# Token routing of a two-part mixture of experts in groups of 512 tokens, the second time inside the attention's last steps

## The reference

```
x = x + 0.5 * ffn(layernorm(x))
x = x + attention(layernorm(x))
x = x + 0.5 * ffn(layernorm(x))        # the same weights as the first

ffn(x):   logits = x @ gate_w                       # 256 x 8 experts
          probs = softmax(logits); take the best 2 of 8, weights made to sum to 1
          for each token and chosen expert e:  silu(x @ w1[e]) * (x @ w3[e]) @ w2[e]
attention(x): a gated delta rule with 16 key heads and 32 value heads of 128, a causal
          convolution of 4 taps ahead of it, a gated norm behind it, and a projection W_out
```

## Time and profile before

| | |
|---|---|
| median of 3 runs | 2922.49 us (2917.46 to 2924.52) |
| profiled execution | 2920.82 us, its span 2919.1 us |
| mean granted TensorE clock | 0.962 of full speed |
| TensorE matmul busy | 2688.0 us, 92% of the span |
| VectorE busy | 1930.2 us, 66% |
| ScalarE busy | 1394.6 us, 48% |
| GpSimd busy | 679.9 us, 23% |

### The profile page before, as it was taken

How to read it: one execution, slowest core, us unless ns; L and a number is a source line. 1 busy time by engine, 2 the same in 40 slices (tenths; PEclk the granted TensorE clock), 3 DMA queues, 4 the chain that set the end, 5 groups by cost and what they waited for, 6 DMA issues and landing times. The chain is left out here.

```text
span 2919.1 us, 58298 instructions
## 1 busy us (share of the span) xinstructions
PE 2688.0 (92%) x19346; PEld 1992.1 (68%) x19347; DVE 1930.2 (66%) x3648; ACT 1394.6 (48%) x4441; POOL 679.9 (23%) x937
## 2 busy tenths in 40 slices
PE   4899997558999999999999999999999995899997
PEld 4566665335777777777777777777777774566665
DVE  5122222799999999999999999999977544322221
ACT  0111111435766667666666676676765551111111
POOL 0222221331232231321322322222221101122221
PEclk7999998889999999999999999999999996799999
DMA  4133322355645555555554554554653313132322
GB/s 164 46 81 101 78 52 56 117 172 181 194 146 165 178 159 168 164 164 165 161 178 149 172 165 158 179 163 153 185 142 94 101 55 126 28 91 72 102 65 47
DMA packets 378409, 374.79 MB, mean 128 GB/s; under 512 B 213360, under 2 KB 293744, under 8 KB 378160
## 3 DMA queue, kind: packets, MB, share of 16 engines
q1 hardware_dynamic: 363184, 351.08, 38.6%
q0 software_dynamic: 14976, 20.46, 4.3%
HBM read 234.87 MB, written 138.67 MB: 128 GB/s over the span
## 5 line engine op out<-in xcount | busy, mean ns | idle before, releaser
L548 PE MATMUL f_ps_up<-f_wbuf,f_xgT 128*128 x1248 | 499.8, 544 | 5.2 <-issue 3.2
L643 DVE TENSOR_TENSOR f_h<-f_h,f_ps_up 128x448 f32<-128x448 f32 x156 | 96.9, 621 | 471.6 <-ACT f_h L617 471.6
L617 ACT ACTIVATE f_h<-f_ps_up 128x448 f32<-128x448 f32 x156 | 84.8, 543 | 635.6 <-PE f_ps_up L548 635.6
L548 PEld LDWEIGHTS f_ps_up<-f_wbuf,f_xgT 128*128 128x128 f32 x1248 | 231.4, 192 | 189.5 <-issue 185.0
L1641 DVE SCALAR_TENSOR_TENSOR at_qk<-at_bank,at_taps_qk,at_qk 128x510 f32<-128x510 f32 (+2 forms) x384 | 281.9, 744 | 36.0 <-ACT at_qk L1512 26.9
L1641 DVE SCALAR_TENSOR_TENSOR at_vT<-at_bank,at_taps_v,at_vT 128x510 f32<-128x510 f32 (+2 forms) x384 | 280.4, 744 | 36.3 <-ACT at_vT L1519 27.3
L1314 PE MATMUL at_bank<-xnT,at_w_qk 128*128 128x512 f32 x512 | 254.6, 621 | 25.1 <-DVE at_qk L1641 21.5
L1890 POOL TENSOR_SCALAR at_small<-at_small 128x4 f32<-128x4 f32 x64 | 15.8, 247 | 1119.3 <-ACT at_squares L1546 1119.3
L515 POOL DMA_INDIRECT sums<-f_y,f_row_of x78 | 123.7, 1586 | 584.1 <-DVE f_y L654 579.4
L570 PE MATMUL f_ps_y<-f_wbuf,f_hT 128*128 x1092 | 248.8, 379 | 1.6 <-DVE f_hT L647 1.6
L1339 PE MATMUL at_bank<-at_w_vz,xnT 128*128 128x256 f32 x1024 | 243.5, 381 | 7.3 <-DVE at_vT L1641 7.2
(11 more groups left out here) (231 smaller groups left out, 5626.6 us busy)
## 6 DMA issues: line engine op xcount, KB each, us to landing
f_wbuf<-in_L_ffn_w_dram SPq DMA_DIRECT2D x48, 896.0 KB, 6.9
at_steps_e<-steps_kept SPq DMA_DIRECT2D x64, 512.0 KB, 6.7
mt_kept<-at_mt_made SPq DMA_DIRECT2D x64, 512.0 KB, 4.1
pt_kept<-at_pt_made SPq DMA_DIRECT2D x64, 512.0 KB, 3.1
at_mt<-mt_kept SPq DMA_DIRECT2D x64, 512.0 KB, 4.0
at_pt<-pt_kept SPq DMA_DIRECT2D x64, 512.0 KB, 4.6
ks_kept<-at_ks_made SPq DMA_DIRECT2D x64, 256.0 KB, 2.7
qk_kept<-at_qk SPq DMA_DIRECT2D x64, 256.0 KB, 2.7
```

The costliest lines, as they stand in the source:

```text
L548: last = te.matmul(ps_up[hf][w][:, 0:MH], xgT[b][:, k, :], wbuf[:, bass.ds(off + (w * WSIZE + k * M + hf * MH), MH)], start=(k == 0), stop ...
L643: v.tensor_tensor(part, part, ps_up[hf][1][:, 0:MH], ALU.mult).then_inc(h_ready, 1)
```

## The change

**Routing in groups.** `build_norm` and its block go. A class `Router` holds the pieces of norm, gate and choice for a group g of 512 tokens (four tiles): `stats` and `shift` on VectorE, `root` on GpSimd, `turn` and `logits` on TensorE, `copy` (both halves of `xnT`) and `exp` on ScalarE, `top` and `pick` on VectorE. Their small buffers now belong to the program. x is loaded in four DMAs, each with its own semaphore, the gate right after them, and the block of constants no longer waits for x.

**First part** (`routed` is False): the pieces run inside the routing block, as a pipeline of four groups. SP stores rows and x by group, and loads expert 1's weights after them.

**Second part** (`routed` is True): the pieces are steps of the walk, for the last key head's four units only; `AFTER` grows from 3 to 5 with the new entries of `STAGE`, so two steps are added at the end. The normalized rows stand in `mt_made` and `pt_made`, whose last use is over; transposes go to `inv_bank`, logits to `gen[0]` and `gen[2]`. SP stores rows and x by unit in the walk and waits for them at its end. The routing block of the second part then begins with the weights of experts 0 and 1 and the cast of `best_f`.

**Turned lists**: the list product loads `in_tile` (78 columns) and streams `at_place` (128), so the result has 78 rows and 128 columns. ScalarE copies it to SBUF (`listed`), and TensorE transposes it back.

**Orders**: all five tables of the drain are new. The front's tables stand twice in the file, with the same content. `tab["b"]` shares memory with `tab["g"]`.

```
-            sp.dma_start(x[:], x_dram.rearrange("b (c p) d -> p (b c) d", p=P)).then_inc(c["x_loaded"], 16)
+            for g in range(4):
+                sp.dma_start(x[:, 4 * g:4 * g + 4, :], x_dram[2 * g:2 * g + 2].rearrange("b (c p) d -> p (b c) d", p=P)).then_inc(c["x_loaded"][g], 16)
+            sp.dma_start(c["gate"][:], gate_w.rearrange("(k p) e -> p k e", p=P)).then_inc(c["gate_loaded"], 16)
...
-            pool.wait_ge(c["x_loaded"], 16)
...
+class Router:
...
+    def shift(self, dve, g):
+        v, c = self.nc.vector, self.c
+        dve.wait_ge(self.moments_done, 4 * g + 4)
+        dve.wait_ge(self.rstd_done, 2 * g + 2)
+        for t in self.tiles(g):
+            v.tensor_scalar(self.xn(g)[:, t - 4 * g, :], self.x[:, t, :], c["mv"][:, t, 0:1], c["rstd"][:, t:t + 1],
+                            ALU.subtract, ALU.mult).then_inc(self.xn_ready, 1)
...
+    def turn(self, pe, g):
+        pe.wait_ge(self.xn_ready, 4 * g + 4)
+        at_least(pe, self.xnT_ready, 2 * (g - self.pairs + 1))
+        for k in range(KD):
+            for t in range(4):
+                last = self.nc.tensor.transpose(self.turned[g % self.pairs][k][:, P * t:P * t + P],
+                                                self.xn(g)[:, t, P * k:P * k + P], self.c["ident"][:])
+            last.then_inc(self.turned_ready, 1)
...
+    def logits(self, pe, g):
+        pe.wait_ge(self.c["gate_loaded"], 16)
+        pe.wait_ge(self.xnT_ready, 2 * g + 2)
+        at_least(pe, self.shifted, g - 1)
...
+    def exp(self, act, g):
+        part = self.c["probs"][:, 4 * g:4 * g + 4, :]
+        act.wait_ge(self.shifted, g + 1)
+        self.nc.scalar.activation(part, part, ACT.Exp).then_inc(self.exp_done, 1)
...
@@ routing block, SP @@
+                    if routed:
+                        weight_loads(sp, 1, w1, w2, w3, wbuf, loaded)
+                        return
+                    for g in range(4):
+                        part = slice(512 * g, 512 * g + 512)
+                        sp.wait_ge(router.xn_ready, 4 * g + 4)
+                        sp.dma_start(rows_in[part, :].rearrange("(t p) d -> p t d", p=P), router.xn(g)).then_inc(rows_stored, 16)
+                        sp.wait_ge(c["x_loaded"][g], 16)
+                        sp.dma_start(sums[part, :].rearrange("(t p) d -> p t d", p=P), x[:, 4 * g:4 * g + 4, :]).then_inc(sums_begun, 16)
+                    weight_loads(sp, 1, w1, w2, w3, wbuf, loaded)
@@ routing block, TensorE @@
+                    if not routed:
+                        router.turn(pe, 0)
+                        for g in range(1, 4):
+                            router.turn(pe, g)
+                            router.logits(pe, g - 1)
+                        router.logits(pe, 3)
...
-                            last = nc.tensor.matmul(ps_token[:], at_place[:, i, :], in_tile[:, i],
+                            last = nc.tensor.matmul(ps_listed, in_tile[:, i].rearrange("p k t -> p (k t)"), at_place[:, i, :],
                                                     start=(i == 0), stop=(i == 2 * NT - 1))
-                    last.then_inc(tokens_summed, 1)
+                    last.then_inc(lists_summed, 1)
+                    pe.wait_ge(lists_copied, 1)
+                    nc.tensor.transpose(spare[0][:, 0:2 * TILES], listed[:],
+                                        c["ident"][0:2 * TILES, 0:2 * TILES]).then_inc(tokens_summed, 1)
@@ routing block, ScalarE @@
+                    act.wait_ge(lists_summed, 1)
+                    nc.scalar.copy(listed[:], ps_listed).then_inc(lists_copied, 1)
@@ routing block, VectorE @@
+                        for g in range(4):
+                            dve.wait_ge(c["x_loaded"][g], 16)
+                            router.stats(dve, g)
+                            if g:
+                                router.shift(dve, g - 1)
+                        router.shift(dve, 3)
+                        for g in range(4):
+                            router.top(dve, g)
+                            router.pick(dve, g)
@@ attention @@
+    "sums_out": -3, "ln_stats": -3, "ln_root": -3,
+    "ln_shift": -4, "rows_out": -4, "ln_turn": -4, "ln_copy": -4,
+    "logits": -5, "gate_exp": -5, "pick": -5,
...
+DRAIN_ACT_ORDER = (("weigh", 0), ("gate_qk", 0), ("copy_state",), ("norm",), ("from_state",), ("y_copy", 0),
...
+DRAIN_DVE_ORDER = (("from_state",), ("inv_x", 32), ("conv_qk", 0), ("ln_shift",), ("conv_qk", 1), ("blocks", 0),
+                   ("add", 0), ("shape",), ("add", 1), ("conv_v", 2), ("conv_v", 3), ("scan",), ("inv_x", 64),
...
+                def rows_out(u):
+                    if u[0] != NK - 1:
+                        return
+                    sp.wait_ge(router.xn_ready, 4 * u[1] + 4)
+                    sp.dma_start(rows_in[UT * u[1]:UT * u[1] + UT, :].rearrange("(t p) d -> p t d", p=P), router.xn(u[1])).then_inc(rows_kept[u[1] % 2], 16)
...
+                def ln_shift(u):
+                    if u[0] != NK - 1:
+                        return
+                    if u[1] < 2:
+                        for k in range(2):
+                            dve.wait_ge(s["pt_spilled" if u[1] else "mt_spilled"][k], 16 * (UNITS // 2))
+                    else:
+                        dve.wait_ge(router.turned_ready, 2 * (u[1] - 1))
+                        dve.wait_ge(rows_kept[u[1] % 2], 16)
+                    router.shift(dve, u[1])
```

More of the change, by code:

```diff
@@ L222, in weight_loads, with build_ffn @@
         eng.dma_start(dst.rearrange("p (k m) -> p k m", k=src.shape[1]), src).then_inc(loaded[e % 2], 16)
-def build_ffn(nc, c, x, xnT, gate_w, w1, w2, w3, rows_in, sums, prefix, finish):
+def build_ffn(nc, c, x, xnT, routed, w1, w2, w3, rows_in, sums, prefix, finish):
     ctx = ExitStack()
@@ L441, in _ @@
                 def _(pool):
+                    if not routed:
+                        for g in range(4):
+                            router.root(pool, g)
                     nc.gpsimd.iota(columns_i[:], [[1, P]], base=0, channel_multiplier=0).then_inc(numbers_made, 1)
@@ L683, in build @@
             ("zeros", [P, D], F32), ("iota_i", [P, TILES + 1], I32), ("iota", [P, TILES + 1], F32))}
-        for name in ("x_loaded", "constants_made", "out_stored"):
+        c.update({name: r.sb("rt_" + name, shape, dtype) for name, shape, dtype in (
+            ("stats", [P, NT, 6], F32), ("mv", [P, NT, 2], F32), ("rstd", [P, NT], F32), ("gate", [P, KD, E], F32),
+            ("row", [P, NT], F32), ("probs", [P, NT, E], F32), ("best", [P, NT, 8], F32), ("best_at", [P, NT, 8], U32))})
+        for name in ("gate_loaded", "constants_made", "out_stored"):
             c[name] = r.dma_sem(name)
+        c["x_loaded"] = [r.dma_sem(f"x_loaded{k}") for k in range(4)]
         c["x_back"] = [r.dma_sem(f"x_back{k}") for k in range(4)]
@@ L976 @@
-DRAIN_ACT_ORDER = (("weigh", 0), ("copy_state",), ("from_state",), ("y_copy", 0), ("y_copy", 1), ("norm",),
-                   ("turn", 1), ("turn", 0), ("conv_v", 2), ("conv_v", 3), ("conv_qk", 0), ("gate_v", 2), ("inv_n",),
-                   ("weigh", 1), ("ks",), ("gate_v", 3), ("conv_qk", 1), ("turn_copies", 0), ("gate_qk", 0),
-                   ("gate_qk", 1), ("z_gate", 0), ("z_gate", 1), ("inv_last",), ("turn_copies", 1), ("lift",))
-DRAIN_DVE_ORDER = (("from_state",), ("inv_x", 32), ("blocks", 0), ("add", 0), ("conv_qk", 0), ("blocks", 1),
-                   ("add", 1), ("conv_v", 2), ("conv_v", 3), ("scan",), ("inv_x", 64), ("mix", 0), ("mix", 1),
-                   ("blocks", 2), ("conv_qk", 1), ("join",), ("shape",), ("blocks", 3))
@@ L1089, in build_attention @@
         blocks_kept = dram("blocks_kept", (NK * 2 * P, BLK * BLK))
+        router = Router(nc, r, c, x, xnT, lambda g: (pt_made if g % 2 else mt_made)[:].rearrange("p (t k) m -> p t (k m)", k=KD),
+                        [inv_bank], lambda g: gen[2 * (g % 2)][:, 0:4 * E].rearrange("p (t e) -> p t e", e=E))
+        rows_kept = [r.dma_sem(f"rows_kept{k}") for k in range(2)]
+        sums_begun = r.dma_sem("sums_begun")
         names = ("nw_ready", "qk_projected", "v_projected", "z_projected", "qk_free", "v_free", "z_free",
```

280 lines of the change are left out of this document (165 added, 115 removed).

## The result

The changed kernel took **2874.57 us** (median of four runs, 2872.21 to 2876.78) beside 2922.23 for the kernel before: ratio 0.9839, 95% interval 0.9822 to 0.9856. Run again beside the experiments it took 2877.02 (2872.28 to 2877.79; 0.9847, 0.9830 to 0.9863). The forecast was 2880, range 2866 to 2902. The span of the profiled execution fell from 2919.1 to 2870.0.

A forecast was written before the change was run, and what follows sets the result against it. TensorE was taken as nearly always busy except in the two routing heads, where every engine waits for the one before. Terms −14.5 − 5.8 − 24.2 + 2.2 = −42.3 from 2920.8, plus 1.67 for the median: 2880 us, range 2866 to 2902.

The forecast's parts named there:

- A, the first head: First part, start to cast of `best_f`: four-group pipeline from x's first quarter brings the cast to 32.8 from 47.30, −14.5 us.
- B, the lists: List products in both parts: turned, the clock may rise as in transposes; −2.9 us each, ends −4.9 and +1.0.
- The first rival: Clock stays down in the turned list products; both parts give 1.0 away instead of 2.9 back, 2888 us; chance 0.23.
- C, behind the last addition: Second head moved into the walk: cast at 2451.6 against 2475.81, −24.2 us, with the last addition at 2436.7.
- Ahead of it: Attention's end: two waits gone −5.8, transposes and logits of units 60 and 61 +5.8, `y_copy` about +2 us.
- `y_copy` of the last unit behind an exponential: On ScalarE, unit 63's `y_copy` stands behind unit 60's exponential, which waits for VectorE's maxima: about +2 us.
- the waits of `y_turn`: TensorE's idle 2.88 us twice in the last two steps, waiting for `shape`; both would go, −5.8 us.
- D: Drain's other steps: `norm` ahead of `from_state` delays `y_copy` and `project` 0.2 us in some 11 steps, +2.2 us.
- The stall of the drain: Rival: early `norm` and `shape` wait for late chains, stalling each of 15 steps by 4.6 us, 2947 us; chance 0.05.
- The third rival: The last unit is not hidden: in-order queues hold each other, the head saves half of C, 2892 us; chance 0.08.

The follow-up runs named there:

- e3: The changed kernel with x loaded in one transfer of 2 MB instead of four; 2878.76 us (0.9851).
- e2: The changed kernel with list products not turned, the streamed operand zero-padded to 128 columns, no copy or transpose back; 2876.48 us (0.9840).
- e1: The changed kernel with the list products turned back in both parts (78 columns streamed, no copy or transpose back); 2883.98 us (0.9867).
- e5: The changed kernel with the second norm, gate and choice out of the walk, as a four-group pipeline in the second routing block; 2884.00 us (0.9873).
- e10: The changed kernel with `shape` alone put back behind both additions and `join` on VectorE, `norm` staying early; 2889.14 us (0.9886).
- e4: The changed kernel with both `norm` put back behind `y_copy` on ScalarE and `shape` behind `join` on VectorE; 2886.30 us (0.9872).
- e7: The changed kernel with transposes of the identity, results unread, put into TensorE's idle time (the smaller set); 2873.39 us (0.9836).

## Why the prediction was right, step by step

**A, the first head: right.** Cast at 33.66 for 32.8: start 5.00 for 4.7, first statistics to the last logit 26.2 for 25.5, choice 2.5 for 2.6. The logits took 3.42 us a group, the slow price that bounded the pipeline at 26.3. The first expert product came at 62.05 and did not wait for weights. e3 gives the start's share, 4.4 us; that the other 9.3 come from the four groups is read from the two timelines, and no run takes the grouping alone away.

**B, the lists: right on the clock, the reason left open.** They ended 9.1 and 9.4 us after their start for 10, so the parts gained 4.3 and 3.4 for 2.9. I had gone by the likeness of the turned form to transposes, which load 128 and stream 128 columns; e2 shows the same rise without turning, where 128 columns are streamed as well. The first rival is out. The sentence of the Trainium skill that the prediction weighed (page "TensorE: Matmul & The Clock Gate", section "What's actually happening") does not agree with this place: by it the products would have run alike in both forms and the time would have been that rival's 2888, where e1 and the changed kernel differ by 8.2 us in their two stretches.

**C, behind the last addition: right.** 15.78 us to the cast for 14.9, for the slow clock in the last transposes and logits (1.97 and 3.55, a grant of 0.50). **Ahead of it: one step wrong.** I gave the last addition +2.0 us. Against the first addition of unit 59 it came 0.25 later. The mis-sized term is `y_copy` of the last unit behind an exponential. It did wait there:

```profile
2407.14 1.09 PE L1572 MATMUL at_bank<-ident,at_y 128*128 128x128 f32 x8 [0.28 <-DVE at_y L1947]
2408.07 1.85 PE L216 MATMUL at_bank<-rt_gate,xnT 128*128 128x8 f32 x16
2410.59 5.40 PE L1588 MATMUL at_bank<-at_w_out,at_yT 128*128 128x256 f32 x16 [0.67 <-ACT at_yT L1735]
```

but while ScalarE waited, TensorE did the logits that I had already charged; only 0.67 us was left. Two delays on two engines side by side were added as if one followed the other. Of the waits of `y_turn` 0.28 is left of twice 2.88. e5, which takes out the pieces and the exponential together, puts both at 5.2 us for the 5.8 + 2.0 of the sum; without them the last addition came 4.9 us sooner than before, for 5.8. What I did not see is what e10 shows: without `shape`'s new place the head in the walk would have cost some 13 us more.

**D: right mechanism, too large.** e4 and e10 show the delay, 0.13 us in five steps of nine, for 0.2 in each of some 11. From unit 50 to unit 59 the first additions took 211.52 us before and 211.71 after, the second ones 210.44 and 211.71: 0.2 or 1.3 in all, in one trace of each, for 2.2.

**The rivals.** The stall of the drain did not come, but its mechanism is real: with `norm` alone put back the time was 2950, where the rival had 2947. The agreement is partly luck: I priced 4.6 us a step in 15 steps, and it was 7.2 in some ten, with the lower clock in it. The point of decision was whether `norm` is early enough for GpSimd's roots to be ready between the additions, and the change moves both. The third rival is out: behind the last addition 25.3 of the 26.2 us came.

**Not forecast:** 2.35 us behind the last first-product mark. 1.08 of it are the first 16 products (9.28 before, 8.20 after, and 8.20 in e1): the grant stayed at 0.50 for 6.0 us from their start before, for 3.9 after. Another 1.4 is a wait of the last scatter for the one ahead of it in the trace of before (4.69 us idle, released by that transfer; 3.29 after, released by VectorE). The trace of e7, whose code there is that of the changed kernel, has the same wait:

```profile
2859.97 1.55 POOL L572 DMA_INDIRECT sums<-f_y,f_row_of  x1 [4.66 <-DMA sums<-f_y,f_row_of]
```

So it comes and goes between executions and can't be put down to the change. For the 16 products this stays open, since there is one trace of the kernel before.

On the spans the sum missed by 6.8 us: 4.3 ahead of the last addition (C's double count, D, and scatter), 1.9 from B and 2.35 from the last stretch, less 0.9 each in A and behind the last addition. On the medians it was 3.0 and 5.4.

## What to carry to other kernels

A serial head behind a long loop is best put into the loop's last steps, but then every piece behind it in an in-order queue must be placed anew: here one move without its partner cost 73 us and turned the gain into a loss. When two engines are each delayed, ask whether the delays lie side by side before adding them. And split a first load where its consumer can begin on a piece: the landing of the first piece counts.

## What was not expected of the hardware

Busy is not the same as fast. TensorE was busy without a gap for 13.94 us at a grant of 0.50 with 78 streamed columns, and with 128, in the same place, the grant was 0.98 in the second half. In the padded kernel more arithmetic took 4 us less. In the first head with extra work the grant sank to 0.50 at 19.8 in one trace and at 17.0 in another, both times in the logits, which load 128x128 and stream 8 columns, while TensorE was busy.

In the first part the stretch view gives a grant of 1.00 where the durations speak of the lower level (11 instructions of the list products in 2.3 us, then 21 in 2.0); there the durations are to be believed:

```profile
44.70:47.00 2.30, 2.27 (x11) 2.27 (x12) 2.27 (x3) 0.00 (x0) 0.00 (x0) 1.00 0.00 0
...
49.00:51.00 2.00, 2.00 (x21) 2.00 (x19) 1.97 (x3) 0.00 (x0) 0.00 (x0) 1.00 0.00 0
```
